# A one-core decoder kernel: one order for the two lanes of its first stage, and bf16 one-hots for the token numbers of its expert choice

## The reference, cut to what matters

```python
x = _layernorm(x + _L0_attn_ref(x, ...W_f, b_f, W_i, b_i, W_h, b_h), axis=-1)   # gates f, i from softplus, a scan over the tokens
x = _layernorm(x + _L0_xattn_ref(x, ctx_1024, ...), axis=-1)                    # 16 heads of 8, softmax over 64 context tokens
x = _layernorm(x + _L0_ffn_ref(...), axis=-1)                                   # fake-quantised weights and inputs
```

## Time and profile before

| what | value |
|---|---|
| median of 3 runs | 3302.5 us (3299.12 to 3313.21) |
| run of the profiled execution | 3299.4 us |
| its span, first to last instruction | 3297.6 us |
| PE busy | 2590.8 us, 79% |
| DVE busy | 1697.6 us, 51% |
| ACT busy | 994.5 us, 30% |
| POOL busy | 355.0 us, 11% |
| mean granted clock of TensorE | 0.92 |

### The profile page before, as it was taken

The page is one execution under the profiler, slowest core; times in us unless marked ns, Lnnn a source line. Parts: engine busy times, 40 slices in busy tenths (PEclk is TensorE's granted clock), DMA queues, the critical chain, the costliest instruction groups (busy, mean ns, idle before and its releaser), DMA issues.

```text
span 3297.6 us, 52950 instructions
## 1 busy us (share of the span) xinstructions
PE 2590.8 (79%) x23038; PEld 1856.7 (56%) x23038; DVE 1697.6 (51%) x4037; ACT 994.5 (30%) x1385; POOL 355.0 (11%) x605
## 2 busy tenths in 40 slices
PE   4666468888888887796677789777897777977778
PEld 3444146777777776664555455554555555555554
DVE  5655735565656564612366531665416654166540
ACT  3333312222322232022232432324323243232432
POOL 0111100110011000064110001100001000010000
PEclk8888658999999999898899999989999899998999
DMA  2000000000000000225500000000000000000000
GB/s 83 1 1 1 2 1 1 8 8 3 6 8 8 8 2 7 95 37 98 142 1 1 1 7 0 1 1 1 7 0 1 1 1 7 0 1 1 1 1 26
DMA packets 39354, 48.14 MB, mean 15 GB/s; under 512 B 7169, under 2 KB 36369, under 8 KB 38354
## 3 DMA queue, kind: packets, MB, share of 16 engines
q1 hardware_dynamic: 33490, 40.43, 4.1%
q0 software_dynamic: 5632, 4.33, 1.0%
HBM read 31.81 MB, written 12.91 MB: 14 GB/s over the span
## 4 chain that ended last, share of the span: by engine, by line
PE 55%; DVE 30%; ACT 6%; issue 4%; POOL 3%; DMA 1%; SPq 0%; DVEq 0%; POOLq 0%; ACTq 0%
PE banks L2391 7%; PE banks L865 6%; DVE wide_area L2267 4%; PE banks L2590 4%; DVE wide_area L1745 3%; PE banks L2380 2%; PE banks L1365 2%; PE banks L2165 2%; PE banks L1330 2%; PE banks L1164 2%; DVE xs L894 2%; DVE weights L2084 2%; PE banks L1398 1%; PE banks L1672 1%; PE banks L1658 1%
## 5 line engine op out<-in xcount | busy, mean ns | idle before, releaser
L2590 PE MATMUL banks<-wA 128*128 128x128 f32 x2664 | 365.1, 290 | 4.2 <-ACT xf L926 2.1
L2590 PEld LDWEIGHTS banks<-wA 128*128 128x128 f32 x2664 | 338.4, 204 | 23.5 <-issue 16.1
L886 DVE BATCH_NORM_STATS2 stats<-banks 128x6 f32<-128x128 f32 x208 | 46.4, 286 | 388.3 <-PE banks L865 362.4
L2267 DVE TENSOR_REDUCE wide_area<-banks 128x8 f32<-128x2048 f32 x64 | 146.8, 2293 | 103.8 <-PE banks L2165 103.8
L901 POOL TENSOR_TENSOR rstd<-moments,eps 128x4 f32<-128x4 f32 x56 | 11.1, 199 | 1431.6 <-DVE moments L890 1431.6
L2248 ACT ACTIVATE weights<-banks 128x2048 f32<-128x2048 f32 x64 | 120.1, 1877 | 96.2 <-PE banks L2174 96.2
L1745 DVE TENSOR_REDUCE wide_area<-banks 128x16 f32<-128x1024 f32 x80 | 94.1, 1219 | 53.2 <-PE banks L1658 53.1
L2391 PE MATMUL banks<-wide_area,big 128*128 128x512 f32 x192 | 85.7, 593 | 0.0
L894 DVE TENSOR_SCALAR xs<-banks,moments,rstd 128x128 f32<-128x128 f32 x208 | 70.8, 403 | 27.0 <-POOL rstd L903 25.5
L2084 DVE TENSOR_TENSOR weights<-banks,wC 128x2048 f32<-128x2048 f32 x32 | 72.2, 2287 | 23.9 <-PE banks L1971 23.9
L901 POOL TENSOR_TENSOR smalls<-smalls,eps 128x4 f32<-128x4 f32 x16 | 3.2, 199 | 724.2 <-DVE smalls L890 724.2
(11 more groups left out here) (761 smaller groups left out, 6085.1 us busy)
## 6 DMA issues: line engine op xcount, KB each, us to landing
big<-in_wE SPq DMA_DIRECT2D x1, 4096.0 KB, 12.6
weights<-long_kernel SPq DMA_DIRECT2D x8, 512.0 KB, 7.9
conv<-wide_area SPq DMA_DIRECT2D x16, 256.0 KB, 2.8
wC<-in_wC SPq DMA_DIRECT2D x1, 3012.0 KB, 17.2
wC<-in_wG SPq DMA_DIRECT2D x1, 2971.0 KB, 19.4
big<-in_wT SPq DMA_DIRECT2D x1, 2560.0 KB, 11.2
x_all<-in_xT SPq DMA_DIRECT2D x1, 2048.0 KB, 10.5
total<-spread SPq DMA_DIRECT2D x8, 256.0 KB, 2.2
```

The lines of the kernel that those rows point to most:

```text
L886: dve.bn_stats(m.stats[:, i, :], self.tokens(i)).then_inc(*sg.up("dve", f"stats{i}"))
L2267: return dve.tensor_reduce(m.peaks[:, k % 2, :, :].rearrange("p t (r c) -> p r t c", r=4)[:, :, :, SPARE[j]], m.bank[:, :, :].rearrange("p ...
L2590: pe.matmul(bank[:, 0:P], m.ident, m.ident, start=True, stop=True)
```

## The change

First stage: each lane has one generator for all four passes (`start_pe` and the like), and the string `FIRST` says which lane is advanced (n is lane 0, f lane 1). The idle ticks of lane 1 are gone. The weight quantisation is in lane 1's DVE generator behind its pass 0, so it comes when that lane is advanced for the first time in pass 1; the extremes of a lane's finished group stand behind the first tick of its next pass.

Choice: the token number is kept in two parts. Its partition part (0 to 127) is multiplied into the one-hot of `hi`; its tile part is had by counting: for each slot, how many tiles have a running count of chosen tokens (`scan`) that is not above it (`below`, `tiles`). The one-hots are bf16, made by 16 + 32 operations on 128x256 with a constant each; the products are two halves of 32 in bf16. `BUSY` has 40 instead of 24 products at 'choice rank' and 5 instead of 6 at 'first norm'.

```diff
-        slot, hi, lo, weight = work[0], m.qf[:, 0:n], m.qf[:, n:2 * n], m.af[:, 0:n]
+        slot, hi = work[0], m.qf[:, 0:n]
         dve.tensor_tensor(slot, slot, work[2], ALU.add).then_inc(*rk.up("dve", "slot"))
         dve.wait_ge(*rk.done("dve", "slot", 0))
         dve.tensor_scalar(hi, slot, 1.0 / 32, -31.0 / 64, ALU.mult, ALU.add).then_inc(*rk.up("dve", "hi0"))
@@ -440,33 +439,38 @@
         dve.wait_ge(*rk.done("dve", "hi1", 0))
         dve.tensor_scalar(hi, hi, -MAGIC, None, ALU.add).then_inc(*rk.up("dve", "hi"))
         dve.wait_ge(*rk.done("dve", "hi", 0))
-        dve.scalar_tensor_tensor(out=lo, in0=hi, scalar=-32.0, in1=slot, op0=ALU.mult, op1=ALU.add).then_inc(*rk.up("dve", "lo"))
-        dve.tensor_tensor(weight.rearrange("p (t e) -> p t e", e=EXPERTS), out,
-                          self.token.unsqueeze(2).broadcast_to([P, TILES, EXPERTS]), ALU.mult).then_inc(*rk.up("dve", "weight"))
-        dve.wait_ge(*rk.done("dve", "weight", 0))
-        k = n // self.CHUNKS
-        for c in range(self.CHUNKS):
-            own = slice(c * k, (c + 1) * k)
-            sixteenth = m.sixteenth[c % 2].rearrange("p (n a) -> p n a", a=16)
-            place = m.place[c % 2].rearrange("p (n b) -> p n b", b=32)
-            if c >= 2:
-                dve.wait_ge(*rk.done("pe", f"slots{c - 2}", 0))
-            dve.tensor_tensor(sixteenth, hi[:, own].unsqueeze(2).broadcast_to([P, k, 16]),
-                              self.iota[:, 0:16].unsqueeze(1).broadcast_to([P, k, 16]), ALU.is_equal)\
-               .then_inc(*rk.up("dve", f"sixteenth{c}"))
-            dve.wait_ge(*rk.done("dve", f"sixteenth{c}", 0))
-            dve.tensor_tensor(sixteenth, sixteenth, weight[:, own].unsqueeze(2).broadcast_to([P, k, 16]), ALU.mult)\
-               .then_inc(*rk.up("dve", f"token{c}"))
-            dve.tensor_tensor(place, lo[:, own].unsqueeze(2).broadcast_to([P, k, 32]),
-                              self.iota.unsqueeze(1).broadcast_to([P, k, 32]), ALU.is_equal)\
-               .then_inc(*rk.up("dve", f"place{c}"))
-        dve.wait_ge(*rk.done("pe", f"slots{self.CHUNKS - 1}", 0))
-        dve.tensor_tensor(work[1].rearrange("p (e b) -> p e b", b=32), m.PT[:, 0, 0:n].rearrange("p (e b) -> p e b", b=32),
-                          self.block.unsqueeze(2).broadcast_to([P, EXPERTS, 32]), ALU.mult).then_inc(*rk.up("dve", "own"))
-        dve.wait_ge(*rk.done("dve", "own", 0))
-        dve.tensor_reduce(m.index, work[1].rearrange("p (e b) -> p b e", b=32), AX, ALU.add).then_inc(*rk.up("dve", "index"))
+        dve.scalar_tensor_tensor(out=m.lo, in0=hi, scalar=-32.0, in1=slot, op0=ALU.mult, op1=ALU.add).then_inc(*rk.up("dve", "lo"))
+        dve.scalar_tensor_tensor(out=m.hi, in0=hi, scalar=1.0, in1=work[3], op0=ALU.add, op1=ALU.mult).then_inc(*rk.up("dve", "masked"))
+        dve.wait_ge(*rk.done("dve", "masked", 0))
+        row = self.token[:, 0:1]
+        for a in range(16):
+            dve.tensor_scalar(m.sixteenth[:, :, a * EXPERTS:(a + 1) * EXPERTS], m.hi.rearrange("p (t e) -> p t e", e=EXPERTS), float(a + 1), row, ALU.is_equal, ALU.mult).then_inc(*rk.up("dve", f"sixteenth{a}"))
+        for b in range(32):
+            dve.tensor_scalar(m.place[b // 16][:, b % 16, :], m.lo, float(b), None, ALU.is_equal).then_inc(*rk.up("dve", f"place{b}"))
+
+        cum, tiles = work[0], m.qf[:, 0:TILES]
+        dve.tensor_tensor(cum.rearrange("p (t e) -> p t e", e=EXPERTS), scan, self.column.unsqueeze(1).broadcast_to([P, TILES, EXPERTS]), ALU.mult)\
+           .then_inc(*rk.up("dve", "cum"))
+        dve.wait_ge(*rk.done("dve", "cum", 0))
+        dve.tensor_reduce(tiles, cum.rearrange("p (t e) -> p t e", e=EXPERTS), AX, ALU.add).then_inc(*rk.up("dve", "cum_own"))
+        dve.wait_ge(*rk.done("dve", "cum_own", 0))
+        dve.scalar_tensor_tensor(out=m.below, in0=tiles.unsqueeze(1).broadcast_to([P, 32, TILES]), scalar=self.start,
+                                 in1=self.iota.unsqueeze(2).broadcast_to([P, 32, TILES]), op0=ALU.subtract, op1=ALU.is_le)\
+           .then_inc(*rk.up("dve", "below"))
+        dve.wait_ge(*rk.done("dve", "below", 0))
+        dve.tensor_reduce(m.qf[:, 64:96], m.below, AX, ALU.add).then_inc(*rk.up("dve", "tiles"))
+        own = work[1].rearrange("p (e h b) -> p e h b", h=2, b=16)
+        for h in range(2):
+            dve.wait_ge(*rk.done("pe", f"slots{h}", 0))
+            dve.tensor_tensor(own[:, :, h, :], m.PT[:, h, 0:P].rearrange("p (e b) -> p e b", b=16),
+                              self.column.unsqueeze(2).broadcast_to([P, EXPERTS, 16]), ALU.mult).then_inc(*rk.up("dve", f"own{h}"))
+        dve.wait_ge(*rk.done("dve", "own1", 0))
+        dve.tensor_reduce(m.qf[:, 96:128], work[1].rearrange("p (e b) -> p b e", b=32), AX, ALU.add).then_inc(*rk.up("dve", "within"))
+        dve.wait_ge(*rk.done("dve", "within", 0))
+        dve.scalar_tensor_tensor(out=m.index, in0=m.qf[:, 64:96], scalar=float(P), in1=m.qf[:, 96:128], op0=ALU.mult, op1=ALU.add)\
+           .then_inc(*rk.up("dve", "index"))
         dve.wait_ge(*rk.done("pe", "turned", 0))
-        dve.tensor_copy(m.slots, m.PT[:, 1, 0:32]).then_inc(*rk.up("dve", "slots"))
+        dve.tensor_copy(m.slots, m.O[:, 0:32]).then_inc(*rk.up("dve", "slots"))
...
-        tiles = TILES // self.CHUNKS
-        for c in range(self.CHUNKS):
-            pe.wait_ge(*rk.done("dve", f"place{c}", 0))
-            for t in range(tiles):
-                mm = pe.matmul(m.PT[:, 0, 0:n], m.sixteenth[c % 2][:, t * P:(t + 1) * P], m.place[c % 2][:, t * n:(t + 1) * n],
-                               start=(c == 0 and t == 0), stop=(c == self.CHUNKS - 1 and t == tiles - 1))
-            mm.then_inc(*rk.up("pe", f"slots{c}"))
+        for h in range(2):
+            pe.wait_ge(*rk.done("dve", f"place{16 * h + 15}", 0))
+            for t in range(TILES):
+                tile = slice(t * EXPERTS, (t + 1) * EXPERTS)
+                mm = pe.matmul(m.PT[:, h, 0:P], m.sixteenth[:, t, :],
+                               m.place[h][:, :, tile].rearrange("p b e -> p e b"), start=(t == 0), stop=(t == TILES - 1))
+            mm.then_inc(*rk.up("pe", f"slots{h}"))
         pe.wait_ge(*rk.done("dve", "index", 0))
         for r in range(4):
-            mm = pe.matmul(m.PT[32 * r:32 * r + 32, 1, 0:32], m.index, m.ident[:, r:P:4], start=True, stop=True)
+            mm = pe.matmul(m.O[32 * r:32 * r + 32, 0:32], m.index, m.ident.rearrange("p (i r e) -> p r e i", r=4, e=EXPERTS)[:, r], start=True, stop=True)
         mm.then_inc(*rk.up("pe", "turned"))
...
-BUSY = {..., 'first norm': 6, ..., 'choice rank': 24}
+BUSY = {..., 'first norm': 5, ..., 'choice rank': 40}
+FIRST = "nnffnnfnffnfnfnnfnffnfnfnfnfnfnfnfnfnfnffnnfnffnnnfnnffnfnffnfnfnfnfnfnfnfnfnfnfnnffnfnnfnfnffnfnnffnfnfnfnfnfnnfnfnffnfnfnfnfnfnfnfnfnnfnffnfnfnfnfnfnfnfnfnfnfnnfffnnf"
...
-        m.sixteenth = [gate_blocks[:, i * 1024:(i + 1) * 1024] for i in range(2)]
-        m.place = [m.wide_q[:, 0:4, :].rearrange("p c t -> p (c t)"), cross_keys]
+        m.sixteenth = gate_blocks[:, 0:2048].bitcast(BF16).rearrange("p (t k) -> p t k", t=TILES)
+        m.place = [x.bitcast(BF16).rearrange("p (b n) -> p b n", b=16) for x in (m.wide_q[:, 0:4, :].rearrange("p c t -> p (c t)"), cross_keys)]
+        m.hi, m.lo = m.af[:, 256:384].bitcast(BF16), m.af[:, 384:512].bitcast(BF16)
+        m.below = gate_blocks[:, 2048:3072].rearrange("p (b t) -> p b t", t=TILES)
...
-            yield from idle(LaneRecurrent.TICKS + i * LAG)
+            yield from idle(LaneRecurrent.TICKS)
...
         def first_dve(dve, i, it):
             g = first[i]
-            yield from g.recurrent.dve(dve, it)
-            yield from idle(i * LAG)
+            steps = g.recurrent.dve(dve, it)
+            next(steps)
+            if it:
+                extremes(dve, i, it - 1)
+            yield
+            yield from steps
             yield from g.norm[0].dve(dve, it, g.recurrent.z_ready(it))
             yield from g.cross.dve(dve, it, start_bias)
             yield from g.norm[1].dve(dve, it, g.cross.z_ready(it))
+
+        def extremes(dve, i, it):
+            x, at = m.x_all[:, (2 * it + i) * T:(2 * it + i + 1) * T], 2 * it + i
+            dve.wait_ge(*first[i].norm[1].sig.done("act", "out", it))
+            dve.tensor_reduce(highest[:, at:at + 1], x, AX, ALU.max).then_inc(*extreme[i].up("dve", "high"))
+            dve.tensor_reduce(lowest[:, at:at + 1], x, AX, ALU.min).then_inc(*extreme[i].up("dve", "low"))
+
+        def start_pool(pool, i):
+            for it in range(ITERS // 2):
+                yield from first_pool(pool, i, it)
+
+        def start_pe(pe, i):
+            for it in range(ITERS // 2):
+                yield from first_pe(pe, i, it)
+
+        def start_act(act, i):
+            for it in range(ITERS // 2):
+                yield from first_act(act, i, it)
+
+        def start_dve(dve, i):
+            for it in range(ITERS // 2):
+                yield from first_dve(dve, i, it)
```

(43 more changed lines are left out.)

16 lines of the change are left out of this document (7 added, 9 removed).

## The result

The changed kernel takes 3276.3 us (median of 4 runs, 3273.4 to 3278.4) against 3307.3 for the kernel before on that chip: a ratio of 0.9887 [0.9857, 0.9917], 31 us. The prediction had 3288, some 14 us less than before, with a range of 3276 to 3300; the result lies at its very edge. Run again unaltered on three chips it gave 0.9945 [0.9929, 0.9961], 0.9916 [0.9891, 0.9941] and 0.9919 [0.9902, 0.9936]; the middle of the four is near 0.992, 26 us. So the gain was about twice the predicted one, and it came from the other place: the first stage gave 26 us where 3 were expected, the choice 1.5 where 11 were.

The account below looks back on a forecast made before the run. No engine bounds the whole span: the first stage is bound by its lanes' chains of waits, the choice by VectorE's queue. 3299.4 - 11 (choice) - 3 (stage) = 3285.4, given as 3288 since medians lay 3 higher; range 3276 to 3300.

Parts of the forecast that it names:

- (b): First stage, pass ends: 20 us in passes 0 and 2, 23 to 26 in 1 and 3; all passes summed, -7.4.
- The walk: First stage: each pass's tick order followed with traced durations, over eighty ticks, good to perhaps 7 us.
- Rival 1: First stage: order better, block costs overlap, passes 1 and 3 gain as 0 and 2; stage -14, total 3277; chance 0.22.
- (a): First stage, attention blocks: a block of both lanes costs 14.0 us against 12.2; eight blocks, up to +14.4.
- (c): First stage, pass 1: weight quantisation behind lane 0's first two operations on VectorE delays what follows by 5.3 to 5.7; +5.6.
- rival 3: First stage, passes 0 and 2: four extra table loads not hidden, stage -9, total 3293; chance 0.12.
- The flags' 7.7 us: Choice, VectorE: 16 comparisons at 0.20 us and 32 at 0.14, 3.2 + 4.5 = 7.7 us.
- the half of 32 products: Choice, TensorE: 32 bf16 slot products 0.06 us apart, 1.9 us; 7.7 if a column costs four times as much.
- Rival 2: Choice: slots gain eaten by half-rate flags or the strided operand; choice -3, stage -3, total 3297; chance 0.13.
- the sentence on the slow stride: Choice: with the slow stride of the products' moving operand, the gain is about 0 instead of -11 us.
- The bound of -14: Choice: largest gain given, -14 us, with flags at 0.10 us each.
- the stage's -3: First stage in total: -7.4 + 5.6 = -2, leaned by one to the gain for a shorter clock half level: -3.

Follow-up runs that it names:

- quant_behind: The changed kernel with the first two ticks of pass 1 exchanged, lane 0's first operations before the quantisation: 0.9947 of the kernel before, -17.5 us.
- Lockstep: The changed kernel with FIRST as "nf" * 80, the lanes tick by tick in turn, lane 0 first: 0.9889 of the kernel before, -38.7 us.
- short_steps: The changed kernel with the slot products' moving operand read in stored order, columns turned round in VectorE's read of the result: 0.9889 of the kernel before, -36.4 us.
- short_again: The changed kernel with the slot products' moving operand in stored order, run once more beside the changed kernel: 0.9892 of the kernel before, -38.2 us.

## Why the prediction was wrong

**The step that failed: the ends, (b).** "Where lane 0's transposes stand in front of lane 1's sum (passes 1 and 3)". They stand there in no pass. The walk decoded a string that lacked seven of 168 characters; even in that one they stand so in pass 1 alone. In pass 1 the walk had 46.6 us to lane 0's first turned products, 14.0 to the second, 23.1 for the end and 5.6 for the quantisation, 89.3. The changed kernel took 40.3, 16.8 and 17.9, 75.0 in all, the quantisation included. So the end is 5.2 of the 14.3 us; the misread start of the pass is 6.3, the quantisation 5.6, and the blocks, taken too short, give 2.8 back. Pass 3 has the same pattern: 36.8 to the first turned products where the walk had 43.7.

The costs held in part. With the walk's string run, passes 0 to 2 took 78.6, 90.1 and 81.3 us against 77, 89.3 and 76.8 forecast, so pass 2 was 4.5 off, and the first L1022 came 3.4 us later than before where the walk had the stage 2 sooner. With the true string pass 0, which the missing characters do not touch but for its last two ticks, took 76.4 us against 77.

Rival 1 was right in half of its mechanism: passes 1 and 3 gain as 0 and 2 do, but no block got cheaper. Its 3277 us beside the measured 3276.3 is luck: it had the stage at -14 and the choice at -11, and they gave -26.6 and -1.5. Its 0.22 was too little because the reading of the string was taken as certain, where one exchanged pair of ticks a pass moves the stage by 20 us.

**(a) The blocks.** From norm to norm the changed kernel's second block, a true lockstep, takes 14.1 us as forecast, and 14.5 in the plain order; the first takes 15.9, and 13.2 in the plain order. Between lane 0's two groups of turned products, where the walk had 14.0 in passes 1 to 3, it is 16.8 to 18.9: this term was too small.

**(c) The quantisation.** Its place was misread from the same string. VectorE's timeline of the changed kernel has it (its first line is L131) directly behind lane 1's scaling, and lane 0's first subtraction begins 9.9 us into the pass and is not late.

```profile
94.92 1.37 DVE L900 TENSOR_SCALAR big<-banks,big 128x128 f32<-128x128 f32 x4
96.20 1.08 DVE L131 TENSOR_REDUCE wscales<-wC 128x7 f32<-128x896 f32 x1
```

Put behind lane 0's first operations it cost 3.8 us in the plain order (76.7 against 72.9) and 3.1 in the given one (78.1 against 75.0), where 5.3 to 5.7 were forecast: the size was 1.5 to 2.6 too large. A part of that is 1.4 us: those operations were done 3.4 us into the pass in `quant_behind` and not 4.8.

**The table loads.** There are six in pass 0 and five in pass 2, as against three in pass 1. Lockstep has four and three there, and lane 1's scan starts only 0.9 us sooner in its pass 0 and 0.5 in its pass 2: the loads are hidden but for that, and rival 3 is out.

**The choice.** The flags' 7.7 us were right (7.6). The term mis-sized is the half of 32 products: 1.9 taken, 7.15 measured, beside the 7.7 that the prediction gave as the bound "if a column costs four times as much". The row it went by (four products 0.06 apart) has a moving operand without that step, and the prediction knew the new one to differ from it in this; "nearest row" was the wrong choice between ends four times apart. Rival 2 had the right cause, the strided operand, with -3 for the choice, and the sentence on the slow stride had about 0; it was -1.5. Its total of 3297 was not met, since it kept the stage at -3. With short steps the first gather comes 15.4 us behind the slot number against 26.5 before: 11.1 us, the forecast of 11. The bound of -14 (flags at 0.10 each) does not follow from the walk: the unread products end near 1399 there whatever the flags take, and the two halves behind them keep the slots near 1404.

**The Trainium skill's rule** ("VectorE: DVE Perf Modes", on the fixed extra latency per instruction) would have had an estimated 10.7 us for the 48 flags. The trace has 7.6, so here the overlap seen in the earlier trace rows decides.

**The sum.** Two errors of opposite sign, 23.6 us too little gain in the stage and 9.5 too much in the choice, left a forecast some 14 us too high. By the medians it was 12 to 17 on three chips and 2 on the one with the long first expert. That the result lies inside the range is luck of the same kind. The last us of the stage's -3 was given for the clock; the mean granted clock of the stage is 0.84 before and after, and no run sets that us apart.

## What to carry to other kernels

An order written as a string must be decoded by a program and compared, at the one or two places that decide, with a trace: a single pair of ticks in which a waiting instruction stands in front of a ready one moved this stage by 5 us a pass. Try the plain common order before believing a searched one; here "nf" repeated beat the given string by some 10 us. When a new matmul reads its moving operand with a large step at every column, price it at the slow end, and see whether the layout can be turned round in whatever reads the result.

## What the runs showed of the hardware

- A 128x128 bf16 product whose moving operand steps by 512 bytes at every column takes 0.22 us from start to start, at a granted clock of 0.94 as at 0.50 (the two stretches above); with eight elements side by side per step it takes 0.06 at 1.00 (`short_steps`, `short_again`). So it was not the clock that set the slow pace.
- TensorE's granted clock fell from a mean of 0.94 to 0.50 while the profile shows it busy without a gap on such products; in `short_steps` it was 1.00 through them.
- Sixteen bf16 tensor_scalar of 128x256 go 0.14 us apart with a constant, 0.20 with a per-partition scalar, a second operation and a result written in runs of eight; which of the three costs the 0.06 was not tried.
- ScalarE stood still for 1.4 us at a time with nothing shown that it waited for, and TensorE once for 1.49 (`short_steps`). In the first expert this was so in all seven profiles on two of the chips and in none of the twelve others. What it is stays open. The first expert then takes up to 9.4 us longer, more than a change of a few us in front of it can show against.
